# Unit 1's routed product kept in SBUF in place of its PSUM bank

## The reference

```
x = layernorm(x + causal_convolution(x, t))             # FFT over time, per channel
x = layernorm(x + ffn0(x))
x = layernorm(x + decaying_complex_convolution(x))       # FFT over time in the reference
x = layernorm(x + ffn1(x))

def ffn(x):                                              # H = C = 128, E = 8, K = 2
    shared = (silu(x @ a) * (x @ b)) @ w_shared_out
    wdense = the two largest softmax gates of 8, zero elsewhere
    hid    = silu(x @ c) * (x @ d)
    return shared + sum over e of wdense[:, e] * (hid @ w2[e])
```

## Time and profile before

| | |
|---|---|
| median of three executions | 299.65 us |
| the profiled execution, whole | 299.31 us |
| its span (first to last instruction) | 297.5 us |
| TensorE matmul busy | 275.9 us, 93% |
| VectorE busy | 228.2 us, 77% |
| ScalarE busy | 157.4 us, 53% |
| GpSimd busy | 149.1 us, 50% |
| mean granted TensorE clock | 0.984 of 2.4 GHz |

### The profile page before, as it was taken

How to read it: one execution, slowest core, us unless ns; L and a number is a source line. 1 busy time by engine, 2 the same in 40 slices (tenths; PEclk the granted TensorE clock), 3 DMA queues, 4 the chain that set the end, 5 groups by cost and what they waited for, 6 DMA issues and landing times.

```text
span 297.5 us, 5265 instructions
## 1 busy us (share of the span) xinstructions
PE 275.9 (93%) x1811; PEld 227.2 (76%) x1811; DVE 228.2 (77%) x487; ACT 157.4 (53%) x534; POOL 149.1 (50%) x221
## 2 busy tenths in 40 slices
PE   8599989889996989999999999999999899999993
PEld 7498878568692949695969696979688686978992
DVE  2796999978899958993889598869877783875710
ACT  1219374655653877835764657385646642641332
POOL 4698934882344455576457665746774110110121
PEclk9799999999997999999999999999999999999998
DMA  6993000004985200670085019301930591097102
GB/s 211 381 322 79 1 0 2 0 0 150 422 285 204 83 0 6 248 316 2 6 345 223 0 24 406 143 0 42 426 140 2 198 389 54 4 389 246 43 10 60
DMA packets 16667, 43.61 MB, mean 147 GB/s; under 512 B 1792, under 2 KB 11520, under 8 KB 12416
## 3 DMA queue, kind: packets, MB, share of 16 engines
q1 hardware_dynamic: 15120, 40.51, 36.8%
q10 hardware_dynamic: 1392, 2.76, 2.5%
q0 software_dynamic: 128, 0.00, 0.0%
HBM read 40.91 MB, written 2.36 MB: 145 GB/s over the span
## 4 chain that ended last, share of the span: by engine, by line
PE 38%; POOL 23%; issue 15%; DVE 11%; ACT 7%; DMA 3%; POOLq 0%; SPq 0%; ACTq 0%; DVEq 0%
PE ps L487 12%; PE ps L585 11%; DVE third L1450 4%; DMA third<-in_fwd 3%; POOL second L1113 3%; POOL second L1108 3%; POOL second L1109 3%; POOL rs L1072 3%; POOL second L1101 3%; POOL rs L1091 3%; PE ps L495 2%; POOL second L1102 2%; PE ps L569 2%; POOL ve L1087 2%; PE ps L581 1%
## 5 line engine op out<-in xcount | busy, mean ns | idle before, releaser
L585 PE MATMUL ps<-w_out,third 128*128 128x128 f32 x704 | 89.9, 276 | 0.4 <-DVE third L1450 0.4
L585 PEld LDWEIGHTS ps<-w_out,third 128*128 128x128 f32 x704 | 84.3, 193 | 0.8 <-DVE third L1450 0.8
L1450 DVE TENSOR_TENSOR third<-ps,first 128x512 f32<-128x512 f32 x80 | 49.2, 682 | 0.3
L1068 POOL TENSOR_TENSOR ve<-ssq,eps 128x4 f32<-128x4 f32 x15 | 3.0, 199 | 74.5 <-ACT xy L819 74.5
L787 ACT ACTIVATE first<-ps 128x512 f32<-128x512 f32 x32 | 19.2, 600 | 24.7 <-PE ps L569 14.7
L827 ACT ACTIVATE xy<-ps,rs 128x128 f32<-128x128 f32 x60 | 17.1, 368 | 22.4 <-POOL rs L1072 22.4
L585 PE MATMUL ps<-w_out,second 128*128 128x128 f32 x192 | 26.7, 275 | 0.0
L581 PE MATMUL ps<-w_out,first 128*128 128x128 f32 x128 | 25.0, 277 | 0.0
L585 PEld LDWEIGHTS ps<-w_out,second 128*128 128x128 f32 x192 | 24.0, 192 | 0.0
L1439 DVE TENSOR_TENSOR first<-ps,first 128x512 f32<-128x512 f32 x16 | 11.0, 687 | 16.5 <-PE ps L563 11.9
L581 PEld LDWEIGHTS ps<-w_out,first 128*128 128x128 f32 x128 | 20.3, 194 | 3.9 <-issue 3.9
(11 more groups left out here) (239 smaller groups left out, 597.1 us busy)
## 6 DMA issues: line engine op xcount, KB each, us to landing
first<-gates SPq DMA_DIRECT2D x32, 1024.0 KB, 7.4
out<-xy SPq DMA_DIRECT2D x7, 256.0 KB, 4.2
third<-in_inv ACTq DMA_DIRECT2D x1, 1536.0 KB, 13.0
xy<-in_L_attn_x SPq DMA_DIRECT2D x2, 512.0 KB, 11.3
third<-in_fwd SPq DMA_DIRECT2D x2, 512.0 KB, 12.2
w_out<-in_L_ffn_w SPq DMA_DIRECT2D x2, 512.0 KB
third<-in_fwd ACTq DMA_DIRECT2D x1, 512.0 KB, 4.8
xy<-in_L_attn_x ACTq DMA_DIRECT2D x1, 384.0 KB, 8.5
```

What stands on the lines that cost most here:

```text
L585: last_ = mm(target[:, at], hs[(EXPERTS * n + e) % 16][:, at], w_out[l][:, 1 + e], start=False, stop=(e == EXPERTS - 1))
L1450: tt(hs[(EXPERTS * n + e) % 16], rows[:], wbc[n % 2][:, e], MUL).then_inc(scaled, 1)
```

## The change

Unit 1's routed product is written to xT[6] in SBUF, as unit 0's is written to xT[7], and unit 1's scaled rows read it there. TensorE's second routed product of unit 2 therefore waits for unit 1's product (`h_done`) rather than for unit 1's eight scaled rows (`scaled`). ScalarE's copy into xT[6] waits for these scaled rows before it overwrites the tile.

```
-        routed_ps, h_first = ps[2], xT[GROUPS - 1]
+        routed_ps, h_first = ps[2], [xT[GROUPS - 1], xT[GROUPS - 2]]
...
                 if n == 0:
                     pe.wait_ge(dve_gate, 4)
-                if n == 1:
-                    pe.wait_ge(h_done, 2)
-                if n >= 2:
+                if 1 <= n < 3:
+                    pe.wait_ge(h_done, 2 * n)
+                if n >= 3:
                     pe.wait_ge(scaled, EXPERTS * n)
                 mm(routed_ps[:], w_rin[l][:, P:2 * P], x[:], start=True, stop=True).then_inc(up_done, 1)
...
-                    if norm == 1 and k == GROUPS - 1:
-                        act.wait_ge(scaled, EXPERTS)
+                    if norm == 1 and k >= GROUPS - 2:
+                        act.wait_ge(scaled, EXPERTS * (GROUPS - k))
...
-                    target, up = (routed_ps if n else h_first)[:], routed_ps
+                    target, up = (h_first[n] if n < 2 else routed_ps)[:], routed_ps
                 tt(target, up[:], sil[kind], MUL).then_inc(h_done, 1)
...
-                rows = routed_ps if n else h_first
+                rows = h_first[n] if n < 2 else routed_ps
```

## The result

Twenty executions of the changed kernel have a median of 303.82 us, twenty of the kernel before 299.91. The ratio is 1.0124, with a 95% interval of 1.0100 to 1.0148: 3.7 us slower. The forecast was 302.4 within 300.4 to 303.9.

The account below looks back on a forecast made before the run. The prediction took a chain through VectorE and ScalarE to bound the kernel until TensorE's second transposes, then TensorE. Span 297.5 + 2.2 (hold) + 0.5 (clock) = 300.2, plus 1.8 outside and 0.34 to the median: 302.4 us, range 300.4 to 303.9.

Parts of the forecast that it names:

- The wait is worth nothing: TensorE's L576 of unit 2 starts 2.8 us earlier, but transposes still wait for ScalarE's L762: worth 0, bound 0 to 4.3.
- The hold: GpSimd's two 512-element table sums each hold one of unit 1's L1450 rows on VectorE 1.08 us: 2.2 us, bounds 0 to 2.6.
- The six small sums: GpSimd's six one-element sums behind the table sums, 0.20 us, put at 0 cost.
- the signs: Predicted trace: L576 near 91.3, two rows 1.76 us, L1460 near 97.5, L762's end near 109.0, second transposes near 109.8.
- It reaches the end in full: From L1460 through L762 to TensorE's second transposes the chain has no slack, so the full 2.2 us reach the end.
- The clock: TensorE idles around the transposes, its clock falling to 1.2 GHz somewhere from 106 to 110 us: 0.5 us, bounds 0 to 1.7.
- the clock was back after one such stretch: Reason for taking 0.5 us: before, TensorE's low clock lasted only one stretch of 3.41 us.
- cover a part: Claim that waits on ScalarE between TensorE's pieces hide some low-clock time; a reason for taking 0.5 of 0 to 1.7.
- No change: Rival, 10%: rows out of SBUF lose nothing and TensorE's head start is lost waiting for ScalarE: 299.7 us.
- the gain: Rival, 5%: TensorE's head start reaches the end, L560 of unit 3 and all behind it earlier: 295.4 us.
- the small hold: Rival, 8%: each table sum holds one VectorE row for 0.26 us only, with no clock loss: 300.2 us.
- The costliest clock: Rival, 17%: TensorE's low clock around the transposes costs its full 1.7 us: 303.6 us.

Follow-up runs that it names:

- e5: Against the kernel before: unit 1's product in free PSUM bank ps5, L576's short wait, TensorE filler products in slot 2; 209.0 us from L1439 to end, ratio 1.0044.
- e1: As the change, but unit 1's product goes to free PSUM bank ps5 instead of SBUF; 211.2 us from L1439 to end, ratio 1.0117 to the kernel before.
- e3: The change, with GpSimd's last two table sums cut from 512 to 8 elements; 211.2 us from L1439 to end, ratio 1.0059 to the kernel before.
- e4: The change, with 8, 3 and 1 TensorE filler products ahead of slot 2's transposes and logits; 211.1 us from L1439 to end, ratio 1.0059.
- e11: Against the kernel before: product in ps5, short wait, two ScalarE factor products moved early, 3, 3 and 1 fillers; 206.9 us from L1439 to end, ratio 0.9897.
- e9: Against the kernel before: product in ps5, short wait, two ScalarE factor products moved ahead of unit 0's squares; 209.0 us from L1439 to end, ratio 0.9954.
- e7: Against the kernel before: product in ps5, short wait, all four ScalarE factor products moved later to slot 2; 215.3 us from L1439 to end, ratio 1.0280.
- e8: Against the kernel before: product in ps5, short wait, two of four ScalarE factor products moved later to slot 2; 213.6 us from L1439 to end, ratio 1.0194.

## Why the prediction was right, point by point

- **The wait is worth nothing.** Right: L576 follows L569 at once (92.47, no idle time), TensorE is done with unit 1 early, and then idles 3.07 us for L762. e5's profile shows the worth with everything else taken out: 209.0 against 209.1.
- **The hold.** Right in place, mechanism and size: two rows of 1.76 us, 2.2 us on the way to L1460, from 0.27 us per 128 elements of the sum (1.76 - 0.68 = 1.08, as in the sum of the prediction). e1 and e3 take it away by the two opposite sides, the row's tile and the sum's length. The six small sums cost VectorE nothing, as put. Less the later start of 1.1 us, the signs came out within 0.1 us: L576 at 91.3, L1460 at 97.5, the end of L762 at 109.0, the second transposes at 109.7.
- **It reaches the end in full.** Right: L1460, L762 and the transposes moved by the same 2.2 us, and the stretch behind kept its length.
- **The clock.** Right that it would fall between 106 and 110 (it fell at 109.5) and no longer at 93.7; too small in size. I took 0.5 out of 0 to 1.7, and it measured 1.95. Its first piece came out, 0.46 us for the second transposes (1.10 against 0.64) where I put 0.45, though the earlier trace rows doesn't show the issue share that I worked it out from. The step that failed is "the clock was back after one such stretch": in the stretch of before that I compared with, TensorE was busy 3.00 of 3.41 us at the low clock and the clock came back; here it worked 4.82 of 6.82 between waits on ScalarE, and the low clock lasted for both halves of these 6.82 us. Why it lasted longer is not shown. All that TensorE had on the chain, from the second transposes to the gate product, fell into it. That the waits on ScalarE "cover a part" was wrong too: these waits follow TensorE's own products and cover nothing of them.
- **The rivals.** No change and the gain are out by the interval, the small hold by the rows of 1.76. The costliest clock (303.6) is where the result lies: 299.65 times 1.0124 is 303.4.
- **Luck.** The median of 303.82 lies in the range only by 0.1. The clock's term of 0.5 in place of 1.95 is the whole miss (299.65 + 2.2 + 1.95 = 303.8), and executions of one kernel differ by more than the 0.1. The mechanism held; that the number fell inside the range was in part luck.

## What to carry to other kernels

Before moving an operand from PSUM to SBUF to free a bank, look at what GpSimd runs in those microseconds. Here VectorE's products with two SBUF inputs and GpSimd's table sums took turns, and a product was held for 1.08 of a sum's 1.28 us. Equal medians don't show it; look for the few long ones, and at their neighbours in GpSimd's timeline. And an engine that is released early only to wait at the next link gains nothing: here TensorE even lost its clock there, 2.1 us in e1. Shorten first the chain that it will wait for; if its clock then falls in what wait is left, fillers can be tried, which kept the clock up in e4, e5 and e11.

## What the runs showed of the hardware

In this kernel the clock fell without a long gap too. In e9 TensorE's idle times were 0.98 and 1.46 us with 0.66 us of work between them, and the clock went to 1.2 GHz (0.50 granted) for 6.8 us. In e7, with 0.84 and 1.46, it held there. In e8, with the same 0.98 and 1.46 as e9, it held through the second transposes and fell at 107.3, 1.9 us behind their start: the idle times alone don't say where it falls. And the hold is mutual: GpSimd's sums of one element, beside rows that start every 0.60 us, went from 0.19 to 0.20 us to 0.52 to 0.65 each, while the rows kept their 0.68.
